# Linear attention and a routed FFN: a fourth W1 buffer, table values in groups, ranks and warming products moved

## What is computed

```
xn = layernorm(x)
q, k = elu(xn @ wq + bq) + 1, elu(xn @ wk + bk) + 1 ; v = xn @ wv + bv      # 16 heads of 8
kv = sum_n k v^T per head and batch ; z = 1 / (q . sum_n k + 1e-6)
x = x + (q kv z) @ wo + bo
xn2 = layernorm(x)
logits = xn2 @ Wr ; expert = argmax(logits) ; p_max = max(softmax(logits))   # 8 experts
x = x + p_max * (gelu(xn2 @ W1[expert] + b1[expert]) @ W2[expert] + b2[expert])   # F = 512
```

## Time and profile before

| | us |
|---|---|
| median of 3 runs (lowest to highest) | 116.18 (115.44 to 116.57) |
| the profiled execution | 115.2 |
| its span | 113.5 |
| PE busy in the span | 96.9 (85%) |
| DVE busy | 71.8 (63%) |
| ACT busy | 56.0 (49%) |
| POOL busy | 54.8 (48%) |

### The profile page before, as it was taken

One profiled execution on the slowest core, in us unless ns is written; L12 is line 12 of the kernel. 1 busy time (PEld: TensorE's weight loads), 2 busy tenths in 40 slices (PEclk: granted clock), 3 DMA queues, 4 the chain that ended last, 5 costly groups with the idle time before them and its releaser, 6 DMA issues.

```text
span 113.5 us, 2550 instructions
## 1 busy us (share of the span) xinstructions
PE 96.9 (85%) x700; PEld 80.1 (71%) x702; DVE 71.8 (63%) x310; ACT 56.0 (49%) x190; POOL 54.8 (48%) x84
## 2 busy tenths in 40 slices
PE   4896979999997998766949996989999999999800
PEld 1333677898886983523318996989999999999600
DVE  5799251847797798885597337567676767674110
ACT  3105875574905705204302754586767676767400
POOL 4168881003059567774570043534545454545550
PEclk9999999999999999999596799999999999999996
DMA  2999999910001100210510455610110101000000
GB/s 75 361 321 321 352 291 299 307 26 6 0 0 48 58 25 24 72 48 24 144 50 24 95 122 139 140 56 20 29 43 12 36 23 32 23 32 29 0 0 0
DMA packets 12125, 10.52 MB, mean 93 GB/s; under 512 B 1472, under 2 KB 9920, under 8 KB 12112
## 3 DMA queue, kind: packets, MB, share of 16 engines
q1 hardware_dynamic: 10576, 7.88, 25.2%
q0 software_dynamic: 1248, 2.14, 5.8%
q10 hardware_dynamic: 288, 0.34, 1.0%
HBM read 7.68 MB, written 3.13 MB: 95 GB/s over the span
## 4 chain that ended last, share of the span: by engine, by line
PE 49%; issue 16%; POOL 12%; DVE 7%; ACT 4%; DMA 3%; DVEq 2%; POOLq 1%; ACTq 1%
PE psum L1005 17%; PE psum L1016 15%; POOL routed_rows L335 9%; DMA w_sb<-in_wcat_dram 3%; PE psum L945 3%; PE psum L998 2%; POOL rows L328 2%; PE psum L840 2%; PE psum L852 2%; PE psum L874 2%; DVEq L246 2%; ACT hid L484 2%; POOLq L65 1%; ACT ex L444 1%; DVE w_st L733 1%
## 5 line engine op out<-in xcount | busy, mean ns | idle before, releaser
L342 POOL DMA_INDIRECT out_dram<-slot x23 | 22.3, 972 | 27.8 <-DVE slot L754 27.1
L484 ACT ACTIVATE hid<-psum,b_sb 128x128 f32<-128x128 f32 x92 | 26.3, 370 | 15.6 <-PE psum L1005 15.6
L1005 PE MATMUL psum<-tT,w_st 128*128 128x128 f32 x184 | 26.0, 288 | 0.2 <-ACT tT L479 0.2
L1016 PE MATMUL psum<-w_sb,hid 128*128 x184 | 24.5, 276 | 0.8 <-ACT hid L484 0.8
L1005 PEld LDWEIGHTS psum<-tT,w_st 128*128 128x128 f32 x184 | 23.8, 202 | 0.3 <-ACT tT L479 0.3
L1016 PEld LDWEIGHTS psum<-w_sb,hid 128*128 128x128 f32 x184 | 22.5, 193 | 1.2 <-issue 1.2
L335 POOL DMA_INDIRECT routed_rows<-rows,slot_at x16 | 16.2, 1014 | 7.5 <-issue 5.0
L754 DVE SCALAR_TENSOR_TENSOR slot<-psum,slot 128x128 f32<-128x128 f32 x23 | 8.0, 350 | 16.6 <-PE psum L1016 16.6
L945 PE MATMUL psum<-ones_bf 128*128 128x512 bf16 x49 | 16.7, 492 | 1.6 <-DVE ones_bf L503 1.5
L945 PEld LDWEIGHTS psum<-ones_bf 128*128 128x128 bf16 x51 | 5.9, 119 | 8.6 <-issue 5.1
L733 DVE COPY w_st<-w_sb 128x512 f32 x23 | 9.8, 432 | 3.0 <-PE psum L1005 1.8
(11 more groups left out here) (154 smaller groups left out, 147.3 us busy)
## 6 DMA issues: line engine op xcount, KB each, us to landing
w_sb<-in_W_dram SPq DMA_DIRECT2D x2, 1024.0 KB, 8.3
w_sb<-in_W_dram SPq DMA_DIRECT2D x4, 512.0 KB, 10.4
slot<-routed_rows SPq DMA_DIRECT2D x23, 66.0 KB, 2.0
x_sb<-in_x_dram SPq DMA_DIRECT2D x3, 256.0 KB, 3.9
routed_rows<-pad_rows SPq DMA_DIRECT2D x1, 528.0 KB, 7.4
b_sb<-in_b_dram SPq DMA_DIRECT2D x1, 512.0 KB, 7.2
out_dram<-slot POOLq DMA_INDIRECT x23
w_sb<-in_wcat_dram ACTq DMA_DIRECT2D x1, 264.5 KB, 3.5
```

The lines of the kernel that those rows point to most:

```text
L342: pool.indirect_dma_start(out=out_flat, out_offset=bass.IndirectOffsetOnAxis(ap=slot[:, i, NUMBER:NUMBER + 1].bitcast(U32), axis=0), in_=s ...
L484: act.activation(hid[:, i % 2, c, :], hid_ps[i % 2][:, c * P:(c + 1) * P], ACT.Gelu, bias=b1_sb[:, bass.ds(expert[i] * FC + c, 1)]).then_i ...
L1005: last = pe.matmul(hid_ps[i % 2][:, c * P:(c + 1) * P], w1_st[:, i % W1_RING, c * P:(c + 1) * P], tT[:, i % RING, :], start=True, stop=True)
L1016: last = pe.matmul(y_ps[i % 2][:, 0:D], hid[:, i % 2, c, :], w2_sb[c][:].rearrange("p e d -> p (e d)")[:, bass.ds(expert[i] * D, D)], star ...
```

## The change

- `W1_RING` goes from 3 to 4; DVE copies four W1s and normalises four tiles, all ahead of the late tables. The skip_repeats steps (before: L794 to L797) come behind the first output.
- Late values are loaded in groups of four (`GROUP`), each ahead of the first tile that needs it (tiles 5, 9, 13, 17, 21), on DVE, ACT and PE. DVE loads the early values ahead of `residual(3)`.
- `choose` is split: `first_best` comes earlier. In the loop `slots` stand ahead of `top_probability` and `feature_k`; at the end of attention `slots` and `top_probability` of batch 2 stand ahead of `inverse(3)`. `rank_sums` come ahead of `product_v`, in PSUM bank 5 for batches 0 and 1.
- For batches 2 and 3 DVE scales the logits (`scaled_logits`), ACT takes one exponential for four tiles without a sum, and DVE sums.
- POOL scatters batch 0's and 1's tiles in other groups between the powers and logits.
- The WOR product comes behind `product_v(0)`, its copy behind `copy_v(0)`. `WARM_START` goes from (6, 8) to (7, 5), `WARM_LAST` from (2, 5, 4, 8, 16) to (2, 6, 3, 8, 16).

```diff
@@ -29,8 +29,8 @@
 DEN_EPS = 1e-6
-WARM_START = (6, 8)
-WARM_LAST = (2, 5, 4, 8, 16)
+WARM_START = (7, 5)
+WARM_LAST = (2, 6, 3, 8, 16)
@@ -46,7 +46,8 @@
     RING = 4
-    W1_RING = 3
+    W1_RING = 4
+    GROUP = 4
     H_RING = 4
@@ -131,6 +132,7 @@
         total = sb("total", [P, B, E], F16)
+        lms = sb("lms", [P, T, E])
         ex = sb("ex", [P, T, E])
@@ -181,14 +183,14 @@
         ks_ps = bank(2, 0, ND)
-        rk_ps = bank(0, 0, J * E)
+        rk_ps = [bank(5 if b < B - 2 else 0, 0, J * E) for b in range(B)]
         cnt_ps = bank(0, CNT, E)
...
         woT_ps = bank(1, 0, P)
-        wor_ps = bank(2, 0, E)
+        wor_ps = bank(5, 0, E)
         bo_ps = bank(6, 0, E)
@@ -222,7 +224,7 @@
                                                             sem("onehot_s"), sem("total_s"))
-        exsum_s, prob_s = sem("exsum_s"), sem("prob_s")
+        lms_s, ex_s, exsum_s, prob_s = sem("lms_s"), sem("ex_s"), sem("exsum_s"), sem("prob_s")
         rk_mm, rkm_s, rank_s, slot_at_s, number_s = sem("rk_mm"), sem("rkm_s"), sem("rank_s"), sem("slot_at_s"), sem("number_s")
@@ -242,11 +244,18 @@
-        def tile_values(engine, table, top):
+        def tile_values(engine, table, top, cols=slice(None)):
             return nc.values_load_multi_w_load_instructions(
-                table[0:1, :], engines=[engine], min_val=0, max_val=top,
+                table[0:1, cols], engines=[engine], min_val=0, max_val=top,
                 skip_runtime_bounds_check_because="sums of counts of tokens and tiles, which the shapes bound")[1]
+
+        def late_values(engine, i):
+            g = i - EARLY
+            return tile_values(engine, expert_b, E - 1, slice(g, min(g + GROUP, LATE)))
+
+        def late_group(i):
+            return EARLY <= i < SLOT_TILES and (i - EARLY) % GROUP == 0
@@ -377,14 +386,16 @@
             ln2(0)
+            scatter_rows(0, range(2))
             x_logits(2)
-            scatter_rows(0, range(J // 2))
+            scatter_rows(0, range(2, 3))
             ln2(1)
-            scatter_rows(0, range(J // 2, J))
+            scatter_rows(0, range(3, J))
+            scatter_rows(1, range(2))
             x_logits(3)
-            scatter_rows(1, range(J // 2))
+            scatter_rows(1, range(2, 3))
             ln2(2)
-            scatter_rows(1, range(J // 2, J))
+            scatter_rows(1, range(3, J))
             scatter_rows(2, range(J))
@@ -438,14 +449,16 @@
             def exp_logits(b):
+                if b >= B - 2:
+                    act.wait_ge(lms_s, b - (B - 2) + 1)
+                    act.activation(ex[:, tiles(b), :], lms[:, tiles(b), :], ACT.Exp).then_inc(ex_s, 1)
+                    return
                 act.wait_ge(lm_s, b + 1)
...
-            act.wait_ge(wor_mm, 1)
-            act.copy(w_sb[:, WOR:WOR + E], wor_ps).then_inc(wor_s, 1)
             normalise(0, range(J // 2, J))
@@ -454,6 +467,8 @@
             copy_v(0)
+            act.wait_ge(wor_mm, 1)
+            act.copy(w_sb[:, WOR:WOR + E], wor_ps).then_inc(wor_s, 1)
             for s in range(1, B):
@@ -493,7 +508,8 @@
                     act.wait_ge(late_expert, 1)
-                    expert += tile_values(mybir.EngineType.Activation, expert_b, E - 1)
+                if late_group(i + 1):
+                    expert += late_values(mybir.EngineType.Activation, i + 1)
                 if i + 1 < SLOT_TILES:
@@ -613,7 +629,7 @@
-            def choose(b):
+            def first_best(b):
                 ts = tiles(b)
@@ -622,6 +638,9 @@
                 dve.tensor_reduce(first[:, ts], pick[:, ts, :], AX_X, ALU.max).then_inc(first_s, 1)
+
+            def choose(b):
+                ts = tiles(b)
                 dve.wait_ge(first_s, b + 1)
@@ -630,14 +649,26 @@
+            def scaled_logits(b):
+                ts = tiles(b)
+                dve.wait_ge(rs2_s, b + 1)
+                dve.wait_ge(lm_s, b + 1)
+                dve.tensor_tensor(lms[:, ts, :], lm[:, ts, :], rows[:, ts, SCALE:SCALE + 1].broadcast_to([P, J, E]),
+                                  ALU.mult).then_inc(lms_s, 1)
+
             def top_probability(b):
-                dve.wait_ge(exsum_s, J * (b + 1))
+                if b < B - 2:
+                    dve.wait_ge(exsum_s, J * (b + 1))
+                else:
+                    dve.wait_ge(ex_s, b - (B - 2) + 1)
+                    dve.tensor_reduce(exsum[:, tiles(b)], ex[:, tiles(b), :], AX_X, ALU.add).then_inc(exsum_s, 1)
+                    dve.wait_ge(exsum_s, J * (B - 2) + b - (B - 2) + 1)
                 dve.reciprocal(rows[:, tiles(b), PROB], exsum[:, tiles(b)]).then_inc(prob_s, 1)
...
             def slots(b):
...
                 dve.wait_ge(rk_mm, b + 1)
-                dve.tensor_tensor(rk_m[:, ts, :], rk_ps.rearrange("p (j e) -> p j e", j=J),
+                dve.tensor_tensor(rk_m[:, ts, :], rk_ps[b].rearrange("p (j e) -> p j e", j=J),
                                   onehot[:, ts, :], ALU.mult).then_inc(rkm_s, 1)
@@ -674,23 +705,25 @@
                     route(s - 2)
+                    first_best(s - 2)
                 inverse(s - 1)
...
                     choose(s - 2)
+                    slots(s - 2)
                     top_probability(s - 2)
                 feature_k(s)
-                if s >= 2:
-                    slots(s - 2)
                 feature_q(s)
...
             route(B - 2)
+            first_best(B - 2)
             choose(B - 2)
-            inverse(B - 1)
+            scaled_logits(B - 2)
             slots(B - 2)
             top_probability(B - 2)
+            inverse(B - 1)
             attend(B - 1)
@@ -717,15 +750,16 @@
+            dve.wait_ge(early_expert, 1)
+            expert = list(tile_values(mybir.EngineType.DVE, expert_a, E - 1))
             residual(B - 1)
...
             route(B - 1)
+            first_best(B - 1)
             choose(B - 1)
+            scaled_logits(B - 1)
             slots(B - 1)
             top_probability(B - 1)
-
-            dve.wait_ge(early_expert, 1)
-            expert = list(tile_values(mybir.EngineType.DVE, expert_a, E - 1))
@@ -757,6 +791,9 @@
                 stage_w1(i)
+
+            for i in range(W1_RING):
+                normal_rows(i)
@@ -783,31 +820,33 @@
                                         step_e[:].unsqueeze(2).broadcast_to([P, 2, LATE, E - 1]), ALU.mult))
-            for i in range(3):
-                normal_rows(i)
             late_step(dve.tensor_reduce(stepped_n[:], stepped[:], AX_X, ALU.add))
...
-            late_step(dve.scalar_tensor_tensor(out=again[:], in0=stepped_n[:, 1, :], scalar=last_first[:],
-                                               in1=start_own[:], op0=ALU.add, op1=ALU.subtract))
-            late_step(dve.tensor_scalar(again[:], again[:], part_no[:], 0.0, ALU.add, ALU.is_lt))
-            late_step(dve.tensor_scalar(skip_row[:], again[:], float(SKIP), None, ALU.mult))
+            def skip_repeats():
+                late_step(dve.scalar_tensor_tensor(out=again[:], in0=stepped_n[:, 1, :], scalar=last_first[:],
+                                                   in1=start_own[:], op0=ALU.add, op1=ALU.subtract))
+                late_step(dve.tensor_scalar(again[:], again[:], part_no[:], 0.0, ALU.add, ALU.is_lt))
+                late_step(dve.tensor_scalar(skip_row[:], again[:], float(SKIP), None, ALU.mult))
...
                     dve.wait_ge(late_expert, 1)
-                    expert += tile_values(mybir.EngineType.DVE, expert_b, E - 1)
+                if late_group(i + W1_RING):
+                    expert += late_values(mybir.EngineType.DVE, i + W1_RING)
                 if i + W1_RING < SLOT_TILES:
...
                 output_rows(i)
+                if i == 0:
+                    skip_repeats()
@@ -853,9 +892,7 @@
             def product_k(b):
-                if b == 0:
-                    pe.wait_ge(wor_s, 1)
-                else:
+                if b >= 1:
                     pe.wait_ge(kvd_s, b)
@@ -878,10 +915,15 @@
             def product_nd(b):
...
                 pe.wait_ge(kvd_s, b + 1)
+                if b == 0:
+                    pe.wait_ge(wor_s, 1)
+                    pe.wait_ge(bo_done, 1)
                 if b >= 1:
...
                     pe.wait_ge(lg_s, b)
+                if b >= 2:
+                    pe.wait_ge(rkm_s, b - 1)
                 for j in range(J):
@@ -896,8 +938,6 @@
             def product_o(b):
-                if b == 0:
-                    pe.wait_ge(bo_done, 1)
                 pe.wait_ge(scT_s, b + 1)
@@ -913,11 +953,12 @@
                     pe.wait_ge(rkm_s, b)
-                pe.wait_ge(xnT_s, min(b + 4, B))
+                if b < B - 2:
+                    pe.wait_ge(sc_s, b + 2)
                 pe.wait_ge(onehot_s, b + 1)
...
                 t0 = b * J
-                rk = rk_ps
+                rk = rk_ps[b]
@@ -951,14 +992,12 @@
             keep_warm(WARM_START[1], warm_ps)
-            pe.wait_ge(wr_s, 1)
-            pe.wait_ge(woT_s, 1)
```

(7 more changed lines are left out.)

## The result

The changed kernel takes **109.62 us** (median of 4 runs, 109.47 to 109.88). The kernel before, run beside it on the same chip, took 115.9 (115.44 to 116.57, 4 runs). The ratio is 0.946, with a 95% interval from 0.940 to 0.951: faster, by 6.3 us, where 3.8 were forecast. The profiled executions took 115.2 and 109.51, spans 113.5 and 107.8: 5.7 less.

What follows compares the result with a forecast made beforehand. TensorE bounds half the span; movable time lies in the start, attention's end with the last routing, and the first six tiles. -0.9 - 1.3 - 1.6 = -3.8 from 115.2 gives 111.4, set against the median 112.4 us; range 110.8 to 114.9.

Steps and rivals of the forecast that it cites:

- A: Start up to batch 1's normalisation: later WOR copy and fewer warming products bring it earlier, -1.1 us.
- rival 1: Start: fewer warming products leave TensorE at 1.2 GHz for batch 0's q, k, v; 114.1 us, chance 0.13.
- B: End of attention on VectorE: a separate sum and inverse(3) behind the reciprocal delay attend(3), +0.8 us.
- C: POOL's queue: scatters and logits ahead of ln2(1) make the second power later, of which +0.3 us shows.
- D: VectorE's load of five early values ahead of residual(3): partly hidden in idle time, +0.4 us.
- E: First transpose ahead of the expert tiles: VectorE early, the 16 warming products bind; -0.9 us, A to D included.
- F: First expert tiles: TensorE's idle time goes, so the clock stays at full level, -1.3 us.
- G: Two holes between the second and sixth down products: group loads and a fourth W1 buffer close them, -1.6 us.
- late next: Tile 5's rows, normalised near 65.2 and wanted near 66: slack 0.8, the most an earlier warming end is worth.
- 2, a clock that falls elsewhere: Clock falls in TensorE's idle time around attend(3), or near 60 us all the same; 114.0 us, chance 0.17.
- 3 fell: Rival in the tile loop: the group loads stall it, making the kernel slower, 118.0 us; chance 0.10.
- 4 fell: Rival: next to nothing reaches the end, as B to D double and F stays out; 115.2 us, chance 0.10.

Runs made afterwards that it cites:

- run 11: Kernel before with attention's new order alone: 114.54 us against 116.65, ratio 0.980 (0.973 to 0.988).
- run 9: Kernel before once more, unchanged, for its trace on the chip of runs 1 to 4: 116.73 us, one execution.
- Run 8: Changed kernel with the late values loaded whole again (GROUP = 18): 111.38 us (110.24 to 111.81).
- run 14: Changed kernel with 16 warming products in place of 8 behind batch 3's o product: 109.42 us, ratio 0.953 (0.947 to 0.959).
- run 15: Changed kernel with 8 last warming products in place of 16 and SP's late row addresses in groups of four: 109.67 us (109.12 to 110.08).
- run 5: Changed kernel again, as a control on a second chip: 110.44 us against 115.29, ratio 0.964 (0.956 to 0.972).
- run 13: Changed kernel again, on a third chip: 109.96 us (109.67 to 111.07), ratio 0.958 (0.950 to 0.967).
- run 12: Changed kernel with 8 last warming products, SP's addresses in groups of four, inverse(3) ahead of slots(2): 111.59 us, ratio 0.952 (0.943 to 0.962).
- run 7: Changed kernel with 8 last warming products in place of 16: 109.48 us, ratio 0.954 (0.946 to 0.961).
- run 16: Kernel before with the entry part (as run 2) and 8 last warming products in place of 16: 111.26 us against 115.19, ratio 0.970.
- run 10: Kernel before with start, entry and group loads together, attention as before: 113.56 us, ratio 0.969 (0.958 to 0.980).
- run 1: Kernel before with the start part alone (WARM_START (7, 5), WOR product and copy moved): 114.69 us against 116.93.
- run 2: Kernel before with the entry alone (four W1 buffers, rows ahead of late tables, early load ahead of residual(3), skip_repeats later): 117.34 us against 116.93.
- run 3: Kernel before with the group loads of four values alone: 115.57 us (113.79 to 116.4) against 116.93.
- run 4: Kernel before with 24 warming products behind the last ranks in place of 16: 117.48 us against 116.93.
- Run 6: Changed kernel without the eight warming products behind batch 3's o product: 111.61 us, ratio 0.972 (0.963 to 0.982).

## Why the prediction was wrong

**A, the start, -1.1: right.** The normalisation moved from 11.13 to 10.33 and the 0.44 of idle time behind it is gone; the first ks product went from 16.15 to 14.80. Of these 1.35, 0.24 come from VectorE's moments of the input, which were that much earlier in this execution. The q product of batch 0 took 1.12 in both traces, so rival 1 fell.

**B and C, +0.8 and +0.3: right in sum.** Attend(3) starts directly behind the reciprocal, at 44.62 where it was 45.14: 0.52 earlier behind a start 1.35 earlier, so 0.83 was lost of the 1.1 forecast. The second power came at 34.05, 0.4 late against the start, as said to 0.1. That is the trace's account; in run 11 attend(3) starts 29.83 after the first ks product, 0.6 more than in run 9, which agrees.

**D, +0.4: right.** The load of five took 0.85 from 47.7 on, and residual(3) starts where it ends, at 48.57. The o product ended at 46.94 + 1.09 = 48.03, so 0.54 lies between, where it was 0.11 in the trace before: the load costs 0.43. Batch 3's routing moved by -0.05 all the same, and not by +0.4, since A gave 1.35 and B and C took 0.83: -1.35 + 0.83 + 0.47 = -0.05, where 0.47 is what was lost between attend(3) and residual(3).

**E, the first transpose, -0.9: this is the step that failed, by its size.** The mechanism was right: "Now the 16 warming products bind." But I gave them the 5.30 of one trace, as if their level were a property of the kernel. They took 3.61, and the first transpose came 3.52 earlier, at 55.77 and not at 58.4. Of these 2.63 the products' length is 1.69, their start 0.55 (52.31, forecast 52.86, by the shift of the routing), and 0.39 that the transposes follow them without the 0.24 that I had put in between (recorded ends are modelled). Run 8 shows the same kernel but for the loads with the products at 5.30: first transpose at 57.54, 1.77 later. So at the level that I assumed E would have been about -1.75.

The bound that I wrote myself, -2.9 for all 16 at full level, turns the sum from -3.8 to -5.8, where 5.7 was measured. That it fits so well is luck: E went beyond this bound, by 0.6, and F and G stayed short of their terms by 0.8.

VectorE had to be early for that. It began the rows at 54.70, so the first were ready near 55.0 (an estimate) and not at 56.7: its reciprocal came at 53.23, 0.5 earlier than before, and the four copies took 1.43 and not 4 x 0.43. Rows at 56.7 would have held the transposes back by some 0.9 (an estimate).

The level goes with the idle time ahead of the last ranks, and not with it alone. All traces, idle against the level of the products behind it (before is the first trace of the kernel before):

| idle us | at full level | wholly or partly at the low level |
|---|---|---|
| 0.5 to 1.1 | runs 14, 15 | |
| 1.8 | run 11 | before |
| 2.2 to 2.4 | after, runs 5, 13, 12 | runs 7, 8, 16 |
| 2.85 | run 10 | |
| 4.0 to 4.2 | | runs 1, 2, 3, 4, 6, 9 |

At 4 us it fell every time, at 1.8 to 2.9 in four traces of ten. Runs 11 and 15 count for little in this table: their low stretch lay just ahead, around the o product, and by making that slow it shortened the idle time. Run 6 shows the long idle time as a cause: beside run 5 on the same chip only the products in it were taken away, and all three executions are within 0.13 of each other, 1.2 over run 5. The other side is weaker: run 14's trace is at full level, but so is that of run 13 beside it, and 109.42 and 109.96 are not apart.

The changed kernel's three traces, with 2.2 us, all have the full level. Its executions range from 109.5 to 111.1 over three chips, and in runs 5 and 13 the four above 110.1 have mean granted clocks of 0.964 to 0.979, where the traced ones have 0.991 and 0.990. So a low stretch lay somewhere in them; that it lay in the 16 products isn't shown, and the result's own 109.72 has 0.971 too.

The Trainium skill, TensorE: Matmul & The Clock Gate, section on what is actually happening, has the throttled state as the default, to which an idle engine returns. The gaps of 4 us agree; the ten in the middle show that the length of one gap doesn't tell it.

**F, the clock in the first tiles, -1.3:** measured -0.89. From the first transpose to the second down product it was 59.29 to 65.55, 6.26, and is 55.77 to 61.14, 5.37; the first hidden product takes 1.16 and not 0.95. The size is near, but the reason that I gave, TensorE's idle 1.53, is not shown: in run 9 the first tiles run at full level (1.16) behind an idle 1.42, in run 11 at the low one (2.08) behind 2.56.

**G, the two holes, -1.6:** measured -1.2. Both are closed, which run 3 shows alone. Four values take 0.34, not 0.79: the straight line through five values (0.85) and 18 (1.61) doesn't hold below five. I had costed the loads at nothing, so no term of the sum changed by it. What was "late next", the rows of tile 5, opened one step by 0.42 (0.14 in run 5, 0.27 in run 13): normalised at 63.77 behind the landing, not 65.2, yet wanted earlier still. That "an earlier end of the warming is worth at most as much", 0.8, was wrong: the tables moved with VectorE, SP's load of addresses to 59.29 from the "about 61" of the forecast, so the rows came 1.4 earlier as well. A slack between two chains is no bound when one engine feeds both.

-3.5 - 0.9 - 1.2 = -5.6, against 5.7 in the spans; the rest of the tile row is the same to 0.1. In the medians the gain is 0.6 more: I added 1.0 for the distance between the profiled execution and the median before, but after it was 0.1. So the forecast of 112.4 was missed by 2.8: E 2.6 more, F and G 0.8 less, and 0.9 by that distance. In runs 5 and 13 the gain in medians was 4.8 and 5.2. Run 5's ratio, 0.964 (0.956 to 0.972), has the forecast's 112.4 / 116.18 = 0.967 within its interval, so by how much the forecast missed depends on the executions as well.

**The rivals.** 1 fell. 2, a clock that falls elsewhere, does happen in some executions, at the place it named too: in runs 11 and 15 the low stretch lay around the o product, and run 15's residual(3) stood at 49.73 where run 13 has 49.06. The stretches of run 15 there, whose o product took 2.02 in place of 1.09:

```profile
46.00:47.00 1.00, 1.00 (x6) 0.58 (x6) 0.83 (x7) 0.30 (x1) 0.69 (x2) 1.00 0.00 0
48.00:49.00 1.00, 1.00 (x6) 1.00 (x6) 0.26 (x2) 0.00 (x0) 0.79 (x1) 0.50 0.20 68
```

3 fell (runs 3 and 8). 4 fell, by the size of the gain. Missing was the rival on the good side: the products at full level.

**Open:** why the gap of 2.2 us drops the clock in some executions, what makes the waits for TensorE late on one chip, and whether attention's new order gains anything by itself.

## What to carry to other kernels

Price warming products at both levels, for they are on the path when they stand behind the last wait; keep so few there that the low level is hidden (run 7). Filling the idle time ahead of them (run 14) may do as well, but isn't apart from the changed kernel. Give a term whose bounds are 2 us apart a chance of its own at each end. And before calling the distance between two chains a cap, look whether the engine that gets faster feeds both.

## What the runs showed of the hardware

- The 16 warming products took 3.61 us in each of the six traces that had them at full level (after, runs 5, 10, 11, 13, 14) and 4.87 to 6.09 in the others.
- In the traces of before and after a load of four values takes 0.31 to 0.34 us (median of an engine's five loads, the last of which has two values), one of five 0.73 to 0.85, one of 18 1.41 to 1.63. The loads of five were the first of their engine; whether the count or the place makes them so much longer isn't separated. The Trainium skill, DMA: Bandwidth & Descriptors, section on latency and other measured facts, gives a tensor_load a floor of about 600 ns; the measured 0.31 to 0.34 is below it.
- On one chip an o product's semaphore came some 2.4 us after its recorded end (runs 1 to 4 and 9), and so did a hidden product's in the tile loop (2.47 in runs 2 and 10). In the first trace of the kernel before the residual came 0.11 behind that end; in the changed kernel's 0.54, where VectorE's own load stood between.
